# First expert layer of an eight-stage decoder: from every expert for every token to 79 tiles of sorted token-expert pairs, with two sums in DRAM

## The reference

```python
logits = einsum('bsh,eh->bse', x, router_w) + expert_bias       # 16 experts
top_w, top_idx = top_k(softmax(logits), 4); top_w /= sum(top_w)
act = silu(x @ gate_proj[e]) * (x @ up_proj[e])                 # 256 -> 224, each expert e
out = act @ down_proj[e]                                        # 224 -> 256
x = x + sum over the 4 chosen experts of top_w * out
```

## Time and profile before

| | us |
|---|---|
| runs | 4768.8, 4774.38, 4774.94 (median 4774.38) |
| profiled execution, its time | 4788.41 |
| its span, first to last instruction | 4786.6 |
| TensorE busy in the span | 3923.9 (82%) |
| VectorE, ScalarE, GpSimd busy | 2799.6, 1611.4, 1349.6 |
| mean granted TensorE clock | 0.918 |

### The profile page before, as it was taken

How to read it: one execution, slowest core, us unless ns; L and a number is a source line. 1 busy time by engine, 2 the same in 40 slices (tenths; PEclk the granted TensorE clock), 3 DMA queues, 4 the chain that set the end, 5 groups by cost and what they waited for, 6 DMA issues and landing times. The chain is left out here.

```text
span 4786.6 us, 58979 instructions
## 1 busy us (share of the span) xinstructions
PE 3923.9 (82%) x18543; PEld 2940.0 (61%) x18543; DVE 2799.6 (58%) x7765; ACT 1611.4 (34%) x3960; POOL 1349.6 (28%) x2074
## 2 busy tenths in 40 slices
PE   6999976999997799999999999983999999960230
PEld 4666654555555578888888888872556565640230
DVE  4666654222222788888888888844666666653123
ACT  2444431111111455545455554521444444420000
POOL 0000000000000365455555455540111111116447
PEclk9999986999997999999999999996999999985665
DMA  1000000000000011111111111111000000011240
GB/s 65 0 0 0 0 8 24 12 12 23 12 12 18 20 37 23 41 38 24 36 23 40 35 29 36 24 18 51 1 0 0 0 0 0 0 64 58 60 143 13
DMA packets 198749, 119.39 MB, mean 25 GB/s; under 512 B 122312, under 2 KB 187654, under 8 KB 197520
## 3 DMA queue, kind: packets, MB, share of 16 engines
q1 hardware_dynamic: 181472, 102.85, 8.3%
q0 software_dynamic: 12288, 9.55, 0.7%
q10 hardware_dynamic: 4800, 4.72, 0.3%
HBM read 102.09 MB, written 38.93 MB: 29 GB/s over the span
## 5 line engine op out<-in xcount | busy, mean ns | idle before, releaser
L1630 DVE SCALAR_TENSOR_TENSOR dl_y<-ps,dl_taps,dl_y 128x255 f32<-128x255 f32 (+2 forms) x1536 | 653.0, 474 | 131.4 <-ACT dl_y L1526 127.3
L1361 PE MATMUL ps<-xnT,dl_wkqv 128*128 128x256 f32 x2048 | 543.4, 391 | 33.9 <-DVE dl_lp L1673 26.4
L923 PE MATMUL ps<-xnT,moe_wgu 128*112 x1024 | 447.3, 595 | 5.2 <-DVE moe_ex L963 5.2
L1361 PEld LDWEIGHTS ps<-xnT,dl_wkqv 128*128 128x128 f32 x2048 | 367.9, 193 | 84.0 <-issue 39.2
L923 PEld LDWEIGHTS ps<-xnT,moe_wgu 128*112 128x112 f32 x1024 | 181.9, 178 | 251.3 <-issue 249.3
L362 POOL TENSOR_TENSOR at_rs<-at_ss,mhalf 128x15 f32<-128x15 f32 x32 | 125.5, 3921 | 745.9 <-DVE at_ss L549 745.9
L183 POOL TENSOR_TENSOR ln_rstd<-ln_ve,mhalf 128x4 f32<-128x4 f32 x24 | 24.2, 1010 | 1084.0 <-DVE ln_ve L169 1084.0
L1284 POOL TENSOR_TENSOR dl_rn<-dl_n,mhalf 128x4 f32<-128x4 f32 x128 | 173.7, 1357 | 548.2 <-DVE dl_n L1646 548.2
L448 PE MATMUL ps<-at_shared,at_v 128*128 128x256 f32 (+2 forms) x1280 | 315.9, 380 | 4.6
L989 DVE TENSOR_TENSOR moe_hT<-moe_sg,ps 112x1024 f32<-112x1024 f32 x64 | 78.2, 1221 | 372.6 <-ACT moe_sg L947 372.6
L1526 ACT ACTIVATE dl_y<-ps,dl_taps 128x256 f32<-128x256 f32 x512 | 260.2, 560 | 95.4 <-PE ps L1361 95.4
(11 more groups left out here) (278 smaller groups left out, 8195.3 us busy)
## 6 DMA issues: line engine op xcount, KB each, us to landing
dl_grow<-decay_rows SPq DMA_DIRECT2D x128, 128.0 KB, 3.0
sp_wgu<-in_w1gu SPq DMA_DIRECT2D x12, 768.0 KB, 10.2
dl_wkqv<-in_w1kqv SPq DMA_DIRECT2D x16, 512.0 KB, 4.7
delta_diag<-dl_lp SPq DMA_DIRECT2D x512, 8.0 KB, 1.5
dl_diag<-delta_diag_tt SPq DMA_DIRECT2D x512, 8.0 KB, 1.7
moe_wgu<-in_w0gu SPq DMA_DIRECT2D x16, 448.0 KB, 3.7
slot_rows<-sp_zero SPq DMA_DIRECT2D x4, 1152.0 KB, 8.1
sp_wd<-in_w1d SPq DMA_DIRECT2D x12, 384.0 KB, 11.5
```

The costliest lines, as they stand in the source:

```text
L923: last = nc.tensor.matmul(k.ps[h][0:IC, m, :], wgu[q][h][:, c, m * IC:(m + 1) * IC], k.xnT[:, c, ds(g * (GT * P), GT * P)], start=c == 0, ...
L1361: last = nc.tensor.matmul(bank(h, m // 2, (m % 2) * S, (m % 2 + 1) * S), wkqv[h][:, c, m * P:(m + 1) * P], k.xnT[:, c, u.seq * S:(u.seq + ...
L1630: last = nc.vector.scalar_tensor_tensor(y[h][:, m, back:S], bank(h, m // 2, (m % 2) * S, (m % 2 + 1) * S - back), taps[h][:, m, KC - 1 - b ...
```

## The change

The layer is computed by pairs of token and expert. 2048 tokens with four experts each are 8192 pairs. They are sorted by expert, each expert's pairs are padded to whole tiles of 128, and 79 tiles hold them whatever the routing; tiles left over are computed too, on rows of padding.

1. `ExpertWeights` issues the loads of all 16 experts' weights on SP, in a block of its own ahead of `set_attention`, into SBUF tiles that hold them all.
2. `routed_experts` normalises x into rows. VectorE counts with masks and shifted sums, TensorE with two products by triangular and all-one matrices, so that each pair gets a slot. The inverse, which token stands in a slot, comes from one-hot rows: 8 VectorE operations and 4 products for each of 16 tiles of tokens.
3. The normalised rows and, beside them, 16 gate weights go to DRAM (`expert_rows`, 272 numbers a row). x goes to the first sum, zeros to the second.
4. For each of 79 tiles: GpSimd fetches 128 rows by index (one row number per partition), TensorE transposes them, computes gate and up with the tokens as the stationary side, transposes the product, computes down; ScalarE applies silu, copies and weighs; VectorE copies, picks the tile's gate weight and multiplies; GpSimd adds the 128 result rows to a sum in DRAM by an indirect transfer with an addition, the even tiles to one sum, the odd to the other. TensorE reads the expert's number of each tile into a register to address the weights.
5. The two sums are read back and added into `k.x`.

The order on each queue is written out: GpSimd issues fetch(i), then add(i - 3); TensorE does up(i), the transposes of h for i - 1, the transposes of x for i + 1, down(i - 2).

The diff, cut to its core, with the engines' lists inside `routed_experts` moved to the left and blank lines left out (sp, pool, pe, act and dve are the queues):

```diff
-def experts(k):
-    ...
+class ExpertWeights:
+    def __init__(self, k, st):
+        self.loaded = k.sem("moe_w_loaded")
+        self.gu = k.sb("moe_wgu", [P, E0, DC * 2 * I0], F32, st)
+        self.d = k.sb("moe_wd", [IC, E0, 2 * D], F32, st)
+        with k.nc.Block() as block:
+            @block.sync
+            def _(sp):
+                for e in range(E0):
+                    sp.dma_start(self.gu[:, e, :].rearrange("p (c n) -> p c n", c=DC),
+                                 k.ins["w0gu"][e].rearrange("(c p) n -> p c n", p=P)).then_inc(self.loaded, 16)
+                    sp.dma_start(self.d[:, e, :].rearrange("p (c n) -> p c n", c=2),
+                                 k.ins["w0d"][e].rearrange("(c p) n -> p c n", p=IC)).then_inc(self.loaded, 16)
+def routed_experts(k, weights):
+    ...
+    TILES = (T * TOPK0 + E0 * (P - 1)) // P
+    W = D + E0
+    ROWS = T + P
+    MAGIC = 12582912.0
+    RX, RH, RY = 4, 2, 4
+    ...
+    xtab = nc.dram_tensor("expert_rows", (ROWS, W), F32, kind="Internal").ap()
+    acc = [nc.dram_tensor(f"expert_sums{q}", (ROWS, D), F32, kind="Internal").ap() for q in range(2)]
+    ...
+        layernorm(k, rows[:, :, 0:D])
+    ...
+    sp.dma_start(acc[0][0:T].rearrange("(t p) d -> p t d", p=P), k.x[:, :, :]).then_inc(stored, 16)
+    sp.wait_ge(zeroed, 1)
+    sp.dma_start(acc[1][0:T].rearrange("(t p) d -> p t d", p=P),
+                 zero[:, 0:D].unsqueeze(1).to_broadcast([P, NT, D])).then_inc(stored, 16)
+    for q in range(2):
+        sp.dma_start(acc[q][T:ROWS], zero[:, 0:D]).then_inc(stored, 16)
+    sp.dma_start(xtab[T:ROWS], zero[:, :]).then_inc(stored, 16)
+    sp.wait_ge(weighed, 1)
+    sp.dma_start(xtab[0:T].rearrange("(t p) d -> p t d", p=P), rows[:, :, :]).then_inc(stored, 16)
+    for q in range(2):
+        sp.wait_ge(added[q], 16 * ((TILES + 1 - q) // 2))
+    for b in range(B):
+        for q, to in enumerate((k.x[:, TB * b:TB * b + TB, :], rows[:, TB * b:TB * b + TB, 0:D])):
+            sp.dma_start(to, acc[q][S * b:S * b + S].rearrange("(t p) d -> p t d", p=P)).then_inc(back, 16)
+    def fetch(i):
+        if i >= RX:
+            pool.wait_ge(turned, i - RX + 1)
+            pool.wait_ge(taken, i - RX + 1)
+        nc.gpsimd.indirect_dma_start(
+            out=xs[i % RX][:, :], out_offset=None, in_=xtab,
+            in_offset=bass.IndirectOffsetOnAxis(index[:, i:i + 1], axis=0),
+            bounds_check=ROWS - 1, oob_is_err=True).then_inc(fetched[i % RX], 16)
+    def add(i):
+        pool.wait_ge(y_ready, i + 1)
+        if i >= 2:
+            pool.wait_ge(added[i % 2], 16 * (i // 2))
+        nc.gpsimd.indirect_dma_start(
+            out=acc[i % 2], out_offset=bass.IndirectOffsetOnAxis(index[:, i:i + 1], axis=0),
+            in_=y[i % RY][:, :], in_offset=None, bounds_check=ROWS - 1, oob_is_err=True,
+            compute_op=ALU.add).then_inc(added[i % 2], 16)
+    pool.wait_ge(index_ready, 1)
+    pool.wait_ge(stored, 96)
+    for i in range(TILES + 3):
+        if i < TILES:
+            fetch(i)
+        if i >= 3:
+            add(i - 3)
+    ...
+    for i in range(NT):
+        pe.wait_ge(tiles_made, i + 1)
+        for j in range(TOPK0):
+            last = nc.tensor.matmul(k.ps[0][:, 1, 0:TILES], lanes[i % 4][:, j, :], tiles[i % 4][:, j, :],
+                                    start=i == 0 and j == 0, stop=i == NT - 1 and j == TOPK0 - 1)
+        last.then_inc(placed, 1)
+    pe.wait_ge(weights.loaded, 16 * 2 * E0)
+    pe.wait_ge(ids_ready, 1)
+    expert = {}
+    def turn_x(i):
+        pe.wait_ge(fetched[i % RX], 16 * (i // RX + 1))
+        if i >= 2:
+            pe.wait_ge(x_kept, i - 1)
+        else:
+            pe.wait_ge(index_ready, 1)
+        for c in range(DC):
+            last = nc.tensor.transpose(x_ps(i)[:, c * P:(c + 1) * P], xs[i % RX][:, c * P:(c + 1) * P], k.ident[:, :])
+        last.then_inc(turned, 1)
+    def up(i):
+        expert[i] = pe.value_load(ids[0:1, i:i + 1], min_val=0, max_val=E0 - 1)
+        pe.wait_ge(x_kept, i + 1)
+        if i >= 2:
+            pe.wait_ge(act_ready, i - 1)
+        for c in range(DC):
+            last = nc.tensor.matmul(up_ps(i), xT[i % 2][:, c, :],
+                                    weights.gu[:, ds(expert[i], 1), c * 2 * I0:(c + 1) * 2 * I0].rearrange("p e n -> p (e n)"),
+                                    start=c == 0, stop=c == DC - 1)
+        last.then_inc(up_ready, 1)
+    def turn_h(i):
+        pe.wait_ge(act_ready, i + 1)
+        if i >= 2:
+            pe.wait_ge(h_kept, i - 1)
+        for c in range(2):
+            last = nc.tensor.transpose(h_ps(i)[:, c * P:(c + 1) * P], hh[i % 2][:, c * IC:(c + 1) * IC], k.ident[:, :])
+        last.then_inc(h_turned, 1)
+    def down(i):
+        pe.wait_ge(h_kept, i + 1)
+        if i >= 2:
+            pe.wait_ge(y_ready, i - 1)
+        for c in range(2):
+            last = nc.tensor.matmul(down_ps(i), hT[i % RH][:, c, :],
+                                    weights.d[:, ds(expert[i], 1), c * D:(c + 1) * D].rearrange("p e n -> p (e n)"),
+                                    start=c == 0, stop=c == 1)
+        last.then_inc(down_ready, 1)
+        del expert[i]
+    turn_x(0)
+    for i in range(TILES + 2):
+        if i < TILES:
+            up(i)
+        if 0 <= i - 1 < TILES:
+            turn_h(i - 1)
+        if i + 1 < TILES:
+            turn_x(i + 1)
+        if i >= 2:
+            down(i - 2)
+    ...
+    def silu(i):
+        act.wait_ge(up_ready, i + 1)
+        if i >= 2:
+            act.wait_ge(act_ready, i - 1)
+        nc.scalar.activation(sg[i % 2][:, :], up_ps(i)[:, 0:I0], ACT.Silu).then_inc(silu_done, 1)
+    def keep_h(i):
+        act.wait_ge(h_turned, i + 1)
+        if i >= RH:
+            act.wait_ge(down_ready, i - RH + 1)
+        nc.scalar.copy(hT[i % RH][:, :, :], h_ps(i).rearrange("p (c s) -> p c s", c=2)).then_inc(h_kept, 1)
+    def weigh(i):
+        act.wait_ge(down_ready, i + 1)
+        act.wait_ge(taken, i + 1)
+        if i >= RY:
+            act.wait_ge(added[i % 2], 16 * ((i - RY) // 2 + 1))
+        nc.scalar.activation(y[i % RY][:, :], down_ps(i), ACT.Copy, scale=wcol[:, i:i + 1]).then_inc(y_ready, 1)
+    for i in range(TILES + 2):
+        if 0 <= i - 1 < TILES:
+            keep_h(i - 1)
+        if i < TILES:
+            silu(i)
+        if i >= 2:
+            weigh(i - 2)
+    ...
+    for i in range(NT):
+        if i >= 4:
+            dve.wait_ge(placed, i - 3)
+        for j in range(TOPK0):
+            nc.vector.tensor_scalar(lanes[i % 4][:, j, :], iota[:, :], lo[:, i, j:j + 1], None, ALU.is_equal)
+        for j in range(TOPK0):
+            last = nc.vector.tensor_scalar(tiles[i % 4][:, j, :], iota[:, 0:TILES], hi[:, i, j:j + 1],
+                                           ident_row[:, i:i + 1], ALU.is_equal, ALU.mult)
+        last.then_inc(tiles_made, 1)
+    ...
+    def keep_x(i):
+        dve.wait_ge(turned, i + 1)
+        if i >= 2:
+            dve.wait_ge(up_ready, i - 1)
+        nc.vector.tensor_copy(xT[i % 2][:, :, :], x_ps(i).rearrange("p (c s) -> p c s", c=DC)).then_inc(x_kept, 1)
+    def take_weight(i):
+        dve.wait_ge(fetched[i % RX], 16 * (i // RX + 1))
+        if i >= 2:
+            dve.wait_ge(taken, i - 1)
+        nc.vector.scalar_tensor_tensor(picked[i % 2][:, :], xs[i % RX][:, D:W], 1.0, pick[:, i, :], ALU.mult, ALU.mult,
+                                       accum_out=wcol[:, i:i + 1]).then_inc(taken, 1)
+    def gate(i):
+        dve.wait_ge(silu_done, i + 1)
+        if i >= 2:
+            dve.wait_ge(h_turned, i - 1)
+        nc.vector.tensor_tensor(hh[i % 2][:, :], sg[i % 2][:, :], up_ps(i)[:, I0:2 * I0], ALU.mult).then_inc(act_ready, 1)
+    keep_x(0)
+    for i in range(TILES):
+        take_weight(i)
+        if i + 1 < TILES:
+            keep_x(i + 1)
+        gate(i)
+    dve.wait_ge(back, 32 * B)
+    for b in range(B):
+        xt = k.x[:, TB * b:TB * b + TB, :]
+        nc.vector.tensor_tensor(xt, xt, rows[:, TB * b:TB * b + TB, 0:D], ALU.add).then_inc(joined, 1)
+        ...
         layernorm(k)
-        with k.own_semaphores(""):
+        with ExitStack() as st, k.own_semaphores("_m"):
+            weights = ExpertWeights(k, st)
             set_attention(k)
-        layernorm(k)
-        with k.own_semaphores(""):
-            experts(k)
+            routed_experts(k, weights)
```

More of the change, by code:

```diff
@@ L871, in experts @@
         ex, tot, rtot = sb("ex", [P, NT, TOPK0]), sb("tot", [P, NT]), sb("rtot", [P, NT])
[L872 to L884, removed]
+        eq = sb("eq", [P, NT, TOPK0, E0])
@@ new lines, in routed_experts @@
+        tiles = [sb(f"tiles{i}", [P, TOPK0, TILES]) for i in range(4)]
+        pad_row = sb("pad_row", [P, TILES])
+        index = sb("index", [P, TILES], U32)
+        over = sb("over", [P, TILES, E0])
+        owner = sb("owner", [P, TILES])
+        pick = sb("pick", [P, TILES, E0])
+        ids = sb("ids", [P, TILES], I32)
+        xs = [sb(f"xs{q}", [P, W]) for q in range(RX)]
```

(20 more changed lines are left out.)

160 lines of the change are left out of this document (97 added, 63 removed).

## The result

The changed kernel takes 4874.2 us (median of 4 runs, 4867.3 to 4879.1), the kernel before 4774.7 beside it on the same chip: ratio 1.0207, 95% interval 1.0188 to 1.0226. It is 2.1% slower. Forecast were 4857 us and "slower" with 0.65.

The account below looks back on a forecast made before the run. TensorE bounds the old stage (666 us); the new loop was to be bound by a ring of waits through the queues. 35 + 60 + 26 + 628 - 666 = +83 us, median 4857 us, range 4700 to 5000.

Parts of the forecast that it names:

- the release: In the tile loop, GpSimd's delay from the end of ScalarE's weighing to the add's start: 1.29 us.
- the add's issue: In the tile loop, GpSimd's issuing of the accumulating transfer, priced by the plain scatter's 0.97 us.
- The ring: Tile loop: transposes, down, weighing, add, fetch and landing wait on one another every tile; 7.3 us at full clock, 8.4 at half.
- TensorE sets the pace: Rival for the tile loop: TensorE's own work bounds it, 4.4 us per tile, 355 for the loop, 4584 us; chance 0.05.
- The period: Time per tile in the loop: 7.9 us, bounds 7.1 to 8.5; the loop 628 us with first tiles and drain.
- The clock: TensorE's granted clock in the tile loop: between 1.2 and 2.4 GHz, the middle taken; always low would make the loop 40 us longer.
- Weights ahead of the set attention: Before the set attention: 11.0 MB of expert weights on SP's queue delay its loads, +35 us, bounds 16 and 43.
- Routing: Before the tile loop: counting, slots, one-hot rows, the token table's store and the first fetch, +60 us, bounds 50 to 75.
- the end: After the tile loop: last weighing and add, reading the sums back and eight additions, 26 us, bounds 20 to 35.
- The shorter ring: Rival for the tile loop: release 0.30, landing 1.15, full clock; 5.7 us per tile, 4686 us, faster; chance 0.27.
- The fetch behind the add: Rival on GpSimd's transfer queue: the accumulating add holds up the following fetch; 9.5 us per tile, 4982 us; chance 0.15.
- VectorE held beside the transfers: Rival in the tile loop: VectorE waits beside indirect transfers, 9.7 us per tile, 140 us more, 4997 us; chance 0.05.

Follow-up runs that it names:

- experiments 1, 2: Against the changed kernel: first, GpSimd's fetch one tile earlier, 4549.6 us; second, TensorE's down projection of i-2 ahead of the transposes of i+1, 4696.4 us.
- Experiment 3: The changed kernel with each tile's rows only stored by the indirect transfer, not added to what DRAM holds: 4802.2 us, ratio 1.0054 to the kernel before.
- experiment 5: The changed kernel with six useless TensorE multiplications ahead of every tile's transposes, in its wait for fetched rows: 4823.7 us, ratio 1.0074 to the kernel before.
- Experiment 4: The changed kernel with the experts' weight loads issued behind the set attention's six loads instead of ahead: 4841.1 us, ratio 1.0130 to the kernel before.
- Experiment 7: The changed kernel with the fetch two tiles earlier, add(i) standing behind fetch(i+5): 4500.8 us, ratio 0.9405 to the kernel before.
- experiment 9: The changed kernel with fetch two tiles earlier, weights behind the set attention's loads, and one DRAM sum, each add awaiting the previous: 4569.2 us, ratio 0.9543.
- the first four experiments: Changed kernel with fetch one tile earlier, 4549.6 us; down projection before transposes, 4696.4; scatter without add, 4802.2; weights behind the set attention's loads, 4841.1.
- the five later ones: Changed kernel with TensorE kept busy, 4823.7 us; one sum, 4884.0; fetch two tiles earlier, 4500.8; that plus weights behind, 4463.2; both with one sum, 4569.2.

## Why the prediction was right, and where it was off

The sign, the mechanism and the range held; the median came 17 us over the forecast. That it came so near is luck in part: the release and the add's issue were both mis-sized, and nearly cancel. By its own steps:

- **The ring sets the pace, not TensorE.** Right. Spread over two tiles at either end it gives back 326 or 182 us (experiments 1, 2), and over two or three tiles at GpSimd's end the tiles take what "TensorE sets the pace" promised, 3.24 to 3.84 us, even less than the 4.4 of that rival. It was priced at 4584 us; the order of two queues was all that kept the kernel from it.
- **The period**, 8.24 for 7.9. At full clock 7.50 for 7.3, at half clock 8.57 for 8.4: two terms were mis-sized, in opposite directions. The add's issue took 1.59 us where I took the scatter's 0.97: the sum priced the accumulating form as a plain one, and the range of the loop had no more for its issue. Experiment 3 puts 0.56 of it on the accumulation. The release took 0.81 where the earlier trace rows had 1.29. Landing 1.90 for 1.8, the issue of the fetch 1.06 for 1.00 and the transposes 0.27 for 0.4 are the rest. With 78 turns, 0.34 us is 27 us; the first tiles and the drain took 8.5 us for 12: the loop took 651 for 628.
- **The clock.** I took the middle of the two levels; the period 8.24 lies two thirds of the way from 7.50 to 8.57. By the Trainium skill's page "TensorE: Matmul & The Clock Gate", section "HAM oscillation", every turn would start at the low clock; the trace agrees in the direction, not in full: the turn at 1110 ran its down projection at 1.06 us, the full clock, after a wait of 4.05 us, the one at 1497 at 1.92. The number for it is experiment 5's: 64 us, the whole loop at full clock against the loop as it is.
- **Costed at nothing, and nothing it was:** up, silu and the gate, and the read of the expert number. The read stands in the profile after, in the view of its line: 0.30 us per tile, once 0.50.

```profile
L1048 PEldq TENSOR_LOAD <-moe_ids x79: 295/300/497, 923.5 to 1566.6; - x79
```

The Trainium skill's "DMA: Bandwidth & Descriptors", "Latency and other measured facts", has 0.6 us for it, twice what this trace shows. The terms of the turn at 1103.89 fill its 7.50 us, so neither figure is on the ring. The add's wait for the add two before shows 3.9 us in all, both times at the end.
- **Weights ahead of the set attention**, +39 for +35; from 717.94 on every second one of their issues, nine in all, took 1.9 us, like the row at 737.64, so the six loads of the set attention were issued only from 739.98 on, and landed behind the weights. Experiment 4 gives 37 back.
- **Routing**, +54.5 for +60; **the end**, +27.4 for +26. Both within their bounds.
- **The sum.** For the layer +106 where I had +83: 4 + 23 + 1 - 5. The comparison of medians, +99.6, is kinder to the forecast than the layer's own rows; where the other 6.6 us went is not shown.
- **The rivals.** (The share left out of the range is 0.05 + 0.09 + 0.07 = 0.21, not 0.19.) The shorter ring (0.27) needed 0.30 for the release and 1.15 for the landing; they were 0.81 and 1.90. The fetch behind the add: its landing is the same with and without accumulation (experiment 3). VectorE held beside the transfers: from 1110.50 to 1111.31 its three operations of a tile follow each other without a gap, but GpSimd issues nothing then, so this turn tests little. Experiment 7 does: GpSimd issues there without a pause, the copies still take 424 to 426 ns, and the whole tile takes 3.24 us, which leaves no room for the 9.73 of the earlier trace rows.
- **What would show it** came as written: issues in pairs, the fetch 1.89 us after the add (1.3 was forecast, the same 0.6), then 4.6 to 5.6 us of waiting for the weighing; TensorE's longest wait is for the fetched rows.

## What to carry to other kernels

Cutting work on the busiest engine pays only as far as the next limit, and in a software pipeline that limit can be a ring through in-order queues; here it was opened by their order alone, with the buffers unchanged: follow one tile from its last step through every queue back to the same step of the next tile, and count how many tiles the ring spans. Here one place more between an add and a fetch was worth 326 us, two were worth 383, and with the weights' loads moved as well a change that was 2.1% slower became one 6.8% faster. The worth of a second sum depends on that ring: the same one bought nothing behind it and 106 us once it was out of the way.

## What the runs showed of the hardware

- An indirect transfer that accumulates in DRAM took GpSimd 1.59 us to issue and landed 3.8 us after its issue began; the same rows stored plainly took 1.03 and 2.5. The fetch issued behind it landed 1.9 us after its own issue had ended, either way.
- The release of a waiting indirect issue has a price of its own: 0.81 us after ScalarE's end, 1.0 after the landing of another transfer (experiment 9), where issues that wait for nothing follow in 0.30.
- Adding 211 us of multiplications to TensorE made the kernel 64 us faster, as the granted clock in the loop rose from 0.72 to 0.97 (experiment 5).
- TensorE's read of one number from SBUF into a register took 0.30 us (median of 79).
- An unchanged stage differs from chip to chip: the 128 scatters of the last layer took 166 us from first to last start in all of the first four experiments, on one chip, and in the profile after; they took 174 to 178 in the five later ones, on two others, and 179 in the profile before. The kernel before as a whole took 4778 us on the one and 4790 to 4791 on the others. What makes the difference is not shown. It explains 12.7 us of the difference between layer and span, and none of the verdicts, which are ratios on one chip.
